# Gates of the second layer: blocks side by side in the row halves, and biases as bf16 parts

## What is computed

```python
def gru_cell(x, h, w_ih, w_hh, b_ih, b_hh):
    gi = x @ w_ih.T + b_ih
    gh = h @ w_hh.T + b_hh
    ir, iz, inn = jnp.split(gi, 3, axis=1)
    hr, hz, hn = jnp.split(gh, 3, axis=1)
    r = jax.nn.sigmoid(ir + hr)
    z = jax.nn.sigmoid(iz + hz)
    n = jnp.tanh(inn + r * hn)
    return (1.0 - z) * n + z * h
...
edge_output = gru_cell(node_support, h, w_ih_e, w_hh_e, b_ih_e, b_hh_e)
edge_support = gat(h, A_node, A_edge, W_gat, a_gat)
node_output = gru_cell(edge_support, h, w_ih_n, w_hh_n, b_ih_n, b_hh_n)
```

## Time and profile before

| | us |
|---|---|
| median of three runs | 1512.53 |
| profiled execution | 1514.42 |
| its span on the core | 1512.7 |
| PE busy | 1348.3 (89%) |
| DVE busy | 1198.2 (79%) |
| ACT busy | 981.1 (65%) |
| share of the chain: PE, DVE, ACT, DMA | 49, 21, 11, 9% |

### The profile page before, as it was taken

One profiled execution on the slowest core, in us unless ns is written; L12 is line 12 of the kernel. 1 busy time (PEld: TensorE's weight loads), 2 busy tenths in 40 slices (PEclk: granted clock), 3 DMA queues, 4 the chain that ended last, 5 costly groups with the idle time before them and its releaser, 6 DMA issues.

```text
span 1512.7 us, 18510 instructions
## 1 busy us (share of the span) xinstructions
PE 1348.3 (89%) x6897; PEld 603.3 (40%) x6922; DVE 1198.2 (79%) x1550; ACT 981.1 (65%) x895; POOL 238.0 (16%) x160
## 2 busy tenths in 40 slices
PE   5899999879988799899999999979968888888894
PEld 1433333323334344454454454534423433334353
DVE  4799966677688797867977967548597898999997
ACT  0000088438843587667667667676698899999983
POOL 1000000000000000000000001133133444444552
PEclk9999999999998999999999999989987999999995
DMA  9999779997999755544544542234633546556610
GB/s 334 409 409 409 286 306 409 412 411 278 409 412 412 291 195 206 185 173 166 183 153 169 182 150 98 70 111 148 229 108 99 188 158 214 171 177 211 220 43 28
DMA packets 135888, 348.80 MB, mean 231 GB/s; under 512 B 7732, under 2 KB 57208, under 8 KB 135544
## 3 DMA queue, kind: packets, MB, share of 16 engines
q1 hardware_dynamic: 119968, 329.27, 58.9%
q10 hardware_dynamic: 15832, 18.36, 3.5%
HBM read 329.78 MB, written 17.83 MB: 230 GB/s over the span
## 4 chain that ended last, share of the span: by engine, by line
PE 49%; DVE 21%; ACT 11%; DMA 9%; issue 9%; ACTq 1%; SPq 0%; POOL 0%; DVEq 0%
PE ps L935 16%; PE ps L1046 8%; DMA ring<-in_adjT 5%; PE ps L1062 4%; DMA work<-in_adjT 3%; PE ps L1220 3%; DVE stage_words L2297 2%; DVE ring L2336 2%; ACT work L1792 2%; PE ps L997 2%; PE ps L1123 2%; ACT work L1782 2%; PE ps L865 2%; DVE work L2718 2%; DVE work L2703 2%
## 5 line engine op out<-in xcount | busy, mean ns | idle before, releaser
L1046 PE MATMUL ps<-ring,X 128*64 128x512 f32 x512 | 233.4, 603 | 11.6 <-DVE ring L2336 9.9
L1047 PE MATMUL ps<-work,X 128*64 128x512 f32 x512 | 233.4, 603 | 0.0
L823 POOL TENSOR_TENSOR ring<-ring,work 128x1024 f32<-128x1024 f32 x72 | 170.0, 2361 | 223.8 <-DVE work L2703 222.5
L776 POOL TENSOR_SCALAR work<-ring 128x1024 int16<-128x1024 uint8 x24 | 27.9, 1165 | 981.6 <-DMA ring<-codes 916.0
L1632 ACT ACTIVATE work<-ring 128x2048 f32<-128x2048 f32 x64 | 122.4, 1913 | 80.1 <-DVE ring L2322 29.9
L935 PE MATMUL ps<-ring,work 128*64 128x512 f32 x672 | 158.2, 616 | 17.5 <-DMA ring<-in_adjT 17.5
L2336 DVE TENSOR_SCALAR ring<-ring 128x2048 f32<-128x2048 f32 x64 | 78.3, 1224 | 72.1 <-ACT work L1632 71.6
L1391 ACT ACTIVATE turn_in<-ps 128x512 f32<-128x512 f32 x12 | 7.2, 597 | 188.0 <-PE ps L935 186.7
L1046 PEld LDWEIGHTS ps<-ring,X 128*64 128x64 f32 x512 | 66.7, 138 | 148.6 <-issue 136.3
L1449 ACT ACTIVATE work<-work,code_bias 128x2048 uint8<-128x2048 bf16 (+1 forms) x32 | 62.3, 1947 | 84.3 <-DVE work L2069 72.6
L2033 DVE TENSOR_TENSOR work<-work,ring 128x1024 f32<-128x1024 f32 (+1 forms) x103 | 102.2, 993 | 8.3 <-DMA ring<-in_adjT 6.7
(11 more groups left out here) (377 smaller groups left out, 2759.6 us busy)
## 6 DMA issues: line engine op xcount, KB each, us to landing
ring<-in_adjT SPq DMA_DIRECT2D x88, 2048.0 KB, 14.6
work<-in_adjT SPq DMA_DIRECT2D x28, 2048.0 KB, 17.6
ring<-in_adjT SPq DMA_DIRECT2D x24, 1024.0 KB, 8.8
ring<-in_adjT SPq DMA_DIRECT2D x48, 512.0 KB, 3.9
ring<-codes SPq DMA_DIRECT2D x32, 512.0 KB, 3.8
ring<-in_adjT SPq DMA_DIRECT2D x64, 256.0 KB, 3.1
codes<-work ACTq DMA_DIRECT2D x32, 256.0 KB, 6.1
codes<-work ACTq DMA_DIRECT2D x64, 128.0 KB, 2.8
```

The source lines that it names most:

```text
L823: nc.gpsimd.tensor_tensor(u.edges[:, cols], u.edges[:, cols], u.angle[:, cols], ALU.mult).then_inc(weighted, 1)
L1046: nc.tensor.matmul(ps[0:F, h, :], rows, ring[:, r, 2 * (m % 2) + i, cols], start=start, stop=stop)
L1047: mm = nc.tensor.matmul(ps[F:P, h, :], rows, negs[:, m % 2, i, cols], start=start, stop=stop)
```

## The change

- The constant part of `hidden` goes: the biases (in + hidden for the first two gates, in and half the hidden one for the third) are split into three bf16 parts, put in rows 64, 0 and 32 of a 65 x 512 bf16 matrix (bias_parts), and added by a bf16 product with a matrix of ones.
- w_hid is loaded into both halves of the partitions (4 more puts) and has no part of zeros: 384 columns instead of 512. hT is [128, 512]: block 2j in the lower 64 partitions, 2j+1 in the upper. The two blocks of a pair are multiplied in the two row halves, into two banks. The order of the gates in a bank is now hidden-new, reset, update, in-new.
- `turn_h` makes 4 transposes of two blocks each; `copy_h` copies 128 x 512 instead of 64 x 1024.
- The pairs of `hidden` stand ahead of and between the two product groups of periods 11 and 12. ACT reads blocks 0 and 1 in period 11, 2 to 5 in period 12, 6 and 7 in period 13; `reset_gate` moves from period 13 to 14.
- DVE makes the parts in `make_weights`: three additions or copies per cell into bias_sum, then seven operations of 512 elements, most behind a step wait. W3_STEPS goes from 6 to 12.

```diff
@@ L102 @@
         mid_w = sb("mid_w", [P, 16 * F])
-        w_hid = mid_w[0:F + 1, 0:8 * F].rearrange("p (g n) -> p g n", g=2)
+        w_hid = mid_w[:, 0:6 * F].rearrange("p (g n) -> p g n", g=2)
+        BIAS_ROWS = F + 1
+        bias_parts = early_w[0:BIAS_ROWS, 0:4 * F].bitcast(BF16)
         winT_sb = mid_w[0:F, 8 * F:11 * F]
@@ L136 @@
         bias_tmp = T2_words[0:F + 1, 0:4 * 3 * F].rearrange("p (i n) -> p i n", i=4)
+        bias_sum = T2_words[F:F + 1, 16 * F:24 * F]
+        bias_next = T2_words[F:F + 1, 24 * F:28 * F].bitcast(BF16)
         w3_pick = T2_words[0:F, 12 * F:14 * F]
@@ L167 @@
         negs = negs_words.rearrange("p (t k c) -> p t k c", t=2, k=2)
-        hT = carve(QC)[0:F + 1, :]
+        hT = carve(HALF)
+        ones_h = carve(HALF)[0:BIAS_ROWS, 0:P // 2].bitcast(BF16)
         shares = gate_words.rearrange("p (c n f) -> p c n f", c=CB, n=2)
@@ L520 @@
-        N_PUTS = 20
-        W3_STEPS, SCALE_STEPS = 6, 7
+        N_PUTS = 24
+        W3_STEPS, SCALE_STEPS = 12, 7
@@ L960 @@
                     pe.wait_ge(rows_read, 2)
-                for c in range(CB):
-                    mm = nc.tensor.transpose(ps[0:F, 6 + c // 4, (c % 4) * P:(c % 4 + 1) * P], X[:, n * CB + c, :],
-                                             ident[:])
+                for j in range(CB // 2):
+                    two = X[:, n * CB + 2 * j:n * CB + 2 * j + 2, :].rearrange("p c f -> p (c f)")
+                    mm = nc.tensor.transpose(ps[:, 6, j * P:(j + 1) * P], two, ident[:])
                 mm.then_inc(hT_ready, 1)
@@ L986 @@
-            def hidden(n, blocks):
+            def hidden(n, j):
-                pe.wait_ge(sums_weighted, n + 1)
-                pe.wait_ge(scores_read, n + 1)
-                for c in blocks:
-                    bank, cols, banks = hid_bank(n, c), slice(c * P, (c + 1) * P), hid_banks(n)
-                    if c >= banks:
-                        pe.wait_ge(hid_read, n * CB + c - banks + 1)
-                    if c == 1 and 2 <= n + 1 < NQ:
+                two = (2 * j, 2 * j + 1)
+                banks = [hid_bank(n, c) for c in two]
+                if j == 0:
+                    pe.wait_ge(sums_weighted, n + 1)
+                    pe.wait_ge(scores_read, n + 1)
+                    if 2 <= n + 1 < NQ:
                         pe.wait_ge(support_read, n)
-                    nc.tensor.matmul(ps[:, bank, :], hT[:, cols], w_hid[:].rearrange("p g n -> p (g n)"),
-                                     start=True, stop=True)
-                    nc.tensor.matmul(ps[:, bank, 0:3 * F], turn_in[:, cols], w_edge[:], start=False, stop=True,
+                if two[1] >= hid_banks(n):
+                    pe.wait_ge(hid_read, n * CB + two[1] - hid_banks(n) + 1)
+                for bank in banks:
+                    nc.tensor.matmul(ps[:, bank, :], ones_h, bias_parts, start=True, stop=True)
+                for i, bank in enumerate(banks):
+                    rows = slice(i * F, (i + 1) * F)
+                    nc.tensor.matmul(ps[:, bank, :].rearrange("p (g n) -> p g n", g=2)[:, :, 0:3 * F],
+                                     hT[rows, j * P:(j + 1) * P], w_hid[rows], start=False, stop=True,
                                      skip_group_check=True)
-                    nc.tensor.matmul(ps[:, bank, 4 * F:7 * F], weighted_in[:, cols], w_att[:], start=False, stop=True,
+                for c, bank in zip(two, banks):
+                    cols = slice(c * P, (c + 1) * P)
+                    nc.tensor.matmul(ps[:, bank, F:4 * F], turn_in[:, cols], w_edge[:], start=False, stop=True,
+                                     skip_group_check=True)
+                    nc.tensor.matmul(ps[:, bank, 5 * F:8 * F], weighted_in[:, cols], w_att[:], start=False, stop=True,
                                      skip_group_check=True).then_inc(hid_ready, 1)
@@ L1082 @@
                         supports(q - 2)
-                    if q and m == 11:
-                        hidden(q - 1, range(4))
-                    if q and m == 12:
-                        hidden(q - 1, range(4, CB))
                     if q == 0 and m % 4 == 0:
                         pe.wait_ge(rest_made[0][0], s // 2 + 1)
+                    hides = q and m in (11, 12)
+                    if hides:
+                        hidden(q - 1, 2 * (m - 11))
                     if m % 2:
                         mask_products(q, m, r)
+                        if hides:
+                            hidden(q - 1, 2 * (m - 11) + 1)
                         edge_products(q, m, r).then_inc(pair_used, 1)
@@ L1198 @@
             turn_rows(2)
-            hidden(3, range(4))
+            for j in range(2):
+                hidden(3, j)
             supports(2)
-            hidden(3, range(4, CB))
+            for j in range(2, CB // 2):
+                hidden(3, j)
             for i in range(4, 10):
@@ L1419 @@
             for g, (wT, b_in, b_hid) in enumerate(((wheT, bie, bhe), (whnT, bin_, bhn))):
-                put(w_hid[0:F, g, 0:2 * F], wT[:, 0:2 * F])
-                put(w_hid[0:F, g, 3 * F:4 * F], wT[:, 2 * F:3 * F])
+                for rows in (slice(0, F), slice(F, P)):
+                    put(w_hid[rows, g, F:3 * F], wT[:, 0:2 * F])
+                    put(w_hid[rows, g, 0:F], wT[:, 2 * F:3 * F])
                 put(bias_tmp[F:F + 1, 2 * g, :], b_in)
@@ L1513 @@
                     act.wait_ge(hid_ready, n * CB)
-                nc.scalar.activation(hT[0:F, :], ps[0:F, 6:8, :].rearrange("p h c -> p (h c)"), ACT.Copy).then_inc(
-                    hT_copied, 1)
+                nc.scalar.activation(hT[:], ps[:, 6, :], ACT.Copy).then_inc(hT_copied, 1)
@@ L1529 @@
                     halves = ps[:, hid_bank(n, c), :].rearrange("p (g n) -> p g n", g=2)
-                    nc.scalar.activation(hid[:, c, :, 0:2 * F], halves[:, :, 0:2 * F], ACT.Tanh, scale=0.5)
-                    nc.scalar.activation(hid[:, c, :, 2 * F:4 * F], halves[:, :, 2 * F:4 * F], ACT.Copy).then_inc(
-                        hid_read, 1)
+                    nc.scalar.activation(hid[:, c, :, F:3 * F], halves[:, :, F:3 * F], ACT.Tanh, scale=0.5)
+                    outer, raw = (a.rearrange("p g (k f) -> p g k f", f=F)[:, :, 0::3, :] for a in (hid[:, c], halves))
+                    nc.scalar.activation(outer, raw, ACT.Copy).then_inc(hid_read, 1)
@@ L1651 @@
                     if q and m == 11:
-                        read_hidden(q - 1, range(4))
+                        read_hidden(q - 1, range(2))
                     if q and m == 12:
-                        read_hidden(q - 1, range(4, CB))
+                        read_hidden(q - 1, range(2, 6))
+                    if q and m == 13:
+                        read_hidden(q - 1, range(6, CB))
                     if q >= 2 and m == 13:
@@ L1949 @@
                 V.tensor_scalar(turn_w[:, 2, F:P], cheb_sb[:, 3, :], 2.0, None, ALU.mult)
+                step = steps_on(own_steps)
                 for g in range(2):
-                    V.memset(w_hid[0:F, g, 2 * F:3 * F], 0.0)
+                    V.tensor_scalar(w_hid[:, g, 0:F], w_hid[:, g, 0:F], 0.5, None, ALU.mult)
                     b_in, b_hid = bias_tmp[F:F + 1, 2 * g, :], bias_tmp[F:F + 1, 2 * g + 1, :]
-                    V.tensor_tensor(w_hid[F:F + 1, g, 0:2 * F], b_in[:, 0:2 * F], b_hid[:, 0:2 * F], ALU.add)
-                    V.tensor_copy(w_hid[F:F + 1, g, 2 * F:3 * F], b_in[:, 2 * F:3 * F])
-                    V.tensor_scalar(w_hid[F:F + 1, g, 3 * F:4 * F], b_hid[:, 2 * F:3 * F], 0.5, None, ALU.mult)
-                    V.tensor_scalar(w_hid[0:F, g, 3 * F:4 * F], w_hid[0:F, g, 3 * F:4 * F], 0.5, None, ALU.mult)
-                step = steps_on(own_steps)
+                    sums = bias_sum[:, 4 * g * F:4 * (g + 1) * F]
+                    V.tensor_scalar(sums[:, 0:F], b_hid[:, 2 * F:3 * F], 0.5, None, ALU.mult)
+                    V.tensor_tensor(sums[:, F:3 * F], b_in[:, 0:2 * F], b_hid[:, 0:2 * F], ALU.add)
+                    ins = V.tensor_copy(sums[:, 3 * F:4 * F], b_in[:, 2 * F:3 * F])
+                step(ins)
+                step(V.memset(bias_parts, 0.0))
+                step(V.tensor_copy(bias_parts[F:F + 1, :], bias_sum))
+                step(V.tensor_tensor(bias_sum, bias_sum, bias_parts[F:F + 1, :], ALU.subtract))
+                step(V.tensor_copy(bias_next, bias_sum))
+                step(V.tensor_tensor(bias_sum, bias_sum, bias_next, ALU.subtract))
+                V.tensor_copy(bias_parts[0:1, :], bias_next)
+                V.tensor_copy(bias_parts[32:33, :], bias_sum)
                 for rows, mean in ((w3_sb, w3_words[0:F, F:F + 1]), (b3_sb[:], b3_mean)):
@@ L2150 @@
             own_link = small[:, 9]
-            reset, update, new_in, new_hid = (hid[:, :, :, i * F:(i + 1) * F] for i in range(4))
+            new_hid, reset, update, new_in = (hid[:, :, :, i * F:(i + 1) * F] for i in range(4))
@@ L2352 @@
                     if q == 0 and m == 11:
```

(8 more changed lines are left out.)

## The result

| | before | after |
|---|---|---|
| median, 22 runs each | 1514.82 us | 1521.42 us |
| all runs | 1510.57 to 1521.4 | 1514.15 to 1524.69 |
| profiled execution: span, time | 1512.7, 1514.42 | 1521.1, 1522.85 |

The ratio is 1.0036, 95% interval [1.0022, 1.0049]: 5.5 us slower (3.3 to 7.4), inside 1% as forecast. The forecast difference was +1.9 us, and the range held the time. The direction is right, with too small a start in the sum.

The account below looks back on a forecast made before the run. PE was taken to bound layer 1, and a delay at the start to go all the way down. Layer 1 -5.1 and start +7.0 gave +1.9 us on the 1512.53 us median: 1514.5 us, range 1504 to 1523.

Parts of the forecast that it names:

- DMA +3.3: Start: four more puts add 256 packets to ACT's queue, so the last constant lands 3.3 us later (0 to 5.1).
- DVE +3.4: Start: seven new 512-element operations and step waits in make_weights delay PE by 3.4 us (2.5 to 4.6).
- Clock +0.3 (0 to 1.5): Start: PE comes back at 1.2 GHz as before, with a somewhat longer slow stretch: +0.3 us (0 to +1.5).
- Start +7.0 (2.5 to 11): Whole start: later constants, DVE's extra operations and PE's slow stretch together cost 7.0 us (2.5 to 11).
- A pair 2.61 us, -6.5 for 16: Layer 1 hidden phase: a pair of blocks takes 2.61 us instead of 3.02; 16 pairs give -6.5 us (-9.8 to +0.5).
- Transposes nothing: Start of each quarter: four feature transposes instead of eight count as nothing, at most -0.4 us in each of four quarters.
- Reads even, slots +0.6, reset gate +0.6 in Q3 only: Layer 1: waits for ACT's reads unchanged; hidden work in four places +0.6 us; moved reset gate +0.6, quarter 3 only.
- Layer 1 -5.1: Layer 1 in all: pair savings less the costs of the new order give -5.1 us (-11 to +2.5).
- rival B: Layer 1: row halves don't overlap, a pair takes 3.05 us or more; +8.9 us, 1521.5 us; chance 0.10.
- A: Start is absorbed while the gates' gain comes: -6 us, 1506.5 us; chance 0.16.
- C: Layer 1: DVE or ACT late in three quarters, 1.5 us each; +4.5 on the sum, 1519 us; chance 0.10.
- D: Something outside moves, as the granted clock from 1094 to 1463 us; either sign, 15 us for 4 hundredths; chance 0.08.

Follow-up runs that it names:

- e1_puts: The kernel before with only the four extra puts, into rows that nothing reads: ratio 1.0037 to the kernel before.
- e3b_late_only: The kernel before, old gates kept, with the second layer's gate weights and biases loaded last and prepared after tile 34: ratio 0.9961 to the kernel before.
- e10: The changed kernel with 13 added PE products, results unread, after the masks of tiles 2 and 3 to fill idle time: ratio 1.0041 to the kernel before.
- e4: The changed kernel with pairs, ACT's reads and reset gate back in their old places: ratio 1.0096 to the kernel before.
- e5: The changed kernel with the reset gate split, blocks 0 to 5 in period 13, 6 and 7 in period 14: ratio 0.999 to the kernel before.
- e7: The changed kernel with each block's feature product followed at once by its own edge and attention products, so row halves never meet: ratio 1.0108 to the kernel before.
- e9: The changed kernel with feature products over all 128 rows, no row halves (sums then hold the neighbouring block's features too): ratio 1.003 to the kernel before.
- e3b_again: Second measurement of the kernel before with only the late loading and preparation of the gates' weights and biases: ratio 0.9976 to the kernel before.
- e3_late_gates: The changed kernel with the gates' weights and biases loaded last on their own semaphore and prepared by DVE after tile 34: ratio 0.995 to the kernel before.

## Why the prediction was right or wrong

- **PE decides in layer 1, and a microsecond of the start goes all the way down.** Right: e1_puts delays add_base by 3.8 us, turn_h(0) by 7.1 and the whole by 5.6 (its ratio). In the other direction it can't be seen: of 2 us won at the start of e3b_late_only 2.3 are there at the first turn and none at turn_h(0), because the passage between them was the shortest of all fourteen in the profile of the kernel before.
- **DMA +3.3.** Measured +3.7 and +3.8: sharing the queue's time by packets held for these four puts.
- **DVE +3.4.** From the landing to the masks of tile 3 it was 33.54 to 38.49 before and is 37.24 to 45.53: +3.3. With these two terms add_base of tile 3 starts 7.04 us later, forecast 6.7.
- **Clock +0.3 (0 to 1.5).** This is the step that failed. From add_base to the first turn it was 36.0 us before; the same code took 37.5 (e10), 37.6 (after), 38.7 (e4, e5, e7) and 41.2 (e9): +1.5 to +5.2. I had counted on the slow stretch that stood there already and only lengthened it. What came was a slower return after 8.8 idle us instead of 2.8, and in e4, e5, e7 and e9 a second slow stretch later on. In the changed kernel the half clock stretches L870 from 1.04 to 1.89 us and L850 from 2.63 to 3.60, 1.8 us together; tile 4 gives 0.2 of it back (6.00 instead of 6.20). In e9 (length, busy PE, PEld, DVE, ACT, POOL, clock, DMA share, GB/s):

```profile
56.00:60.00 4.00, 4.00 (x11) 1.21 (x12) 3.92 (x4) 0.00 (x0) 0.00 (x0) 0.50 1.02 410
...
80.00:84.00 4.00, 4.00 (x12) 1.61 (x13) 2.17 (x10) 0.00 (x0) 0.00 (x0) 0.50 0.66 263
```

- **Start +7.0 (2.5 to 11).** At turn_h(0) the six kernels with this start (e10's added products among them) stand at 611.57, 611.59, 611.76, 613.53, 613.80 and 616.42 us, median 612.65: +10.8 on the 601.83 of before. In the changed kernel itself it is +9.9: 3.7 + 3.3 + 1.6 to the first turn, and 1.3 more down to turn_h(0), 524.0 us against 522.7. That last term is in part luck of the one profile of before: all the others take 523.1 or more, whatever their start. At the first turn, ahead of that, the start costs 8.7.
- **A pair 2.61 us, -6.5 for 16.** Bias products 0.45 (forecast 0.46), halves 0.85 (0.84), but edge and attention 1.50 instead of 1.31. I took the 0.2 us of L1220 for the whole drain, where it was the way in; behind it stands a product of another tiling form, so the way out could not be read there. A pair saves 3.02 - 2.79 = 0.23, the 16 pairs 3.7 us, where 0.41 and 6.5 were forecast. By e9, bf16 biases and 384 columns save nothing without the halves (3.04 us): the gain is the overlap less what the two changes of form cost.
- **Transposes nothing.** Four take 0.66 us where eight took 1.06, and quarter 1 adds up only with them: 4 x 0.23 + 0.40 - 0.18 for the slots = 1.14, measured 1.15. I had put this term at nothing, at most -0.4 a quarter. It has no run of its own.
- **Reads even, slots +0.6, reset gate +0.6 in Q3 only.** No wait for a read at the bias products of quarter 1, as forecast, and in quarters 2 and 3 only 0.15 us (at 798.56) where the kernel before waited 0.57 in each; the slots show as 0.54 instead of 0.45 for the biases behind edge products. What the split takes back is 0.5 in Q2 too, and 1.5 in Q3, though PE's wait there fell from 2.11 to 1.55.
- **Layer 1 -5.1.** The three quarters give -5.0 in the two profiles, of which 1.5 is the half-clock moment of before in Q1; the gates are worth 3.5 to 3.7 there. The forecast was for all four groups of pairs, and in these profiles the stage with the fourth is 3.5 us longer (clock 0.92 against 0.94). At equal clock the gates are worth 0.7 to 1.2 there, 4.2 to 4.9 in all. That -5.0 and -5.1 agree is luck.
- **The sum.** By the profiles +9.9, -5.0 and +3.5 are +8.4 us, by the ratio of all runs it is +5.5. The last turn_h stands 5.0 us later than before, where 2 were forecast. How much of the difference over all runs is the start, and how much the lower clock of the changed kernel (median 0.9485), the record doesn't separate; its start alone, 8.7 us at the first turn, less 4.2 to 4.9 leaves 3.8 to 4.5, which is inside the measured 3.3 to 7.4.
- **The time.** 1521.42 us lies in 1504 to 1523, but not in the 1510 to 1518 that had most of the chance; it lies on the 1521.5 of rival B, whose mechanism is out. The base was low, too: the median of three was 1512.53, that of 22 is 1514.82. The width of the range held the time, not the sum.
- **Rivals.** A (the start is absorbed) is out: L870 starts at 50.15. B (no overlap) is out: e7_halves_apart is 1.03 us a pair slower. C (DVE late at the quarter's end) is there in Q2 and Q3, with 2.0 us altogether, a part of the 4.5 I gave it. D (clock in layer 3): the stage takes 378.8 to 386.0 us, with a granted clock from 1085 to 1200 us of 0.85 in the two profiles of before and after and 0.90 in e1_puts. It does so with no order by kernel (e3b_late_only and e3b_again are one program and have 378.83 and 382.44 us). But medians don't average all of it away: the changed kernel's 22 runs have the clock median 0.9485, every other kernel's but e4_old_places (0.948) 0.9515 or more. A part of D thus can't be excluded.

## What to carry to other kernels

Weights that are used late don't belong in the queue that gates the start: here 4 puts and the splitting of the biases cost 7 us in place and the clock's return on top, and moving their loading and preparation behind tile 34 turned a change from +5.5 us to -7.6 (of which 3.6 to 5.9 came by the same move in the kernel before). Cost an excursion into row halves with both changes, here 0.39 us, and ask for at least two products per stay: one alone took 1.04 us here, as long as two, where one over whole rows takes 0.64. Where executions scatter by 10 us, compare stages at equal granted clock, and see that the stages add up to the whole before you explain it: here three quarters of layer 1 looked right while the stage behind them was 3.5 us off.

## What was not expected of the hardware

- A tiling change between whole rows and row halves is paid on the way in (0.20 us) and on the way out (0.19 us).
- The clock after an idle time is not a matter of its length alone. With PE kept busy to 45.9 us, a wait of 4.26 us was followed by 0.50 from 52 to 60 us, the same as one of 8.84 us after slower work; e3_late_gates, with 5.56 us idle in front of tile 3, has 0.65 and 0.50 from 64 to 72 us although PE was busy without a gap from 38 to 64, and then waited only 0.78 us.
- Layer 3 runs in anything from 378.8 to 386.0 us in programs whose layer 3 is the same.
